# The beginning of a fused feed-forward, attention, feed-forward kernel in another order: the first tiles' statistics ahead, down's transposes behind tile 0, a share of the copies and the output bias on VectorE

## The chip, the cores and the metric

The kernel runs on one core of one Trainium2 chip. The metric is the device time of one execution in microseconds; for the kernel before there are three such runs. A trace of one further execution, the profiled one, is what the rows below come from. Engines: PE is TensorE, DVE is VectorE, ACT is ScalarE, POOL is GpSimd, SP is SyncE, which only issues DMAs.

## What is computed

The input x has 16 x 1024 rows of 256 columns, in float32. The layer is a sandwich: half a feed-forward block, attention, half a feed-forward block with the same weights.

```python
def fp4_quant_dequant(x):
    xb = x.reshape(shape[:-1] + (shape[-1] // BLOCK, BLOCK))     # BLOCK = 16
    scale = jnp.max(jnp.abs(xb), axis=-1, keepdims=True) / 6.0
    scale = jnp.maximum(scale, jnp.float32(1e-12))
    xn = xb / scale
    idx = jnp.searchsorted(_MID, jnp.abs(xn))
    q = _GRID[idx] * jnp.sign(xn) * scale
...
gate = fp4_linear(x, w_gate)            # 256 -> 704, x and w quantized
y = fp4_linear(x, w_up)
h = jax.nn.silu(gate) * y
return fp4_linear(h, w_down)            # 704 -> 256
...
x = x + 0.5 * _L0_ffn_ref(_layernorm(x, axis=-1), w_gate, w_up, w_down)
x = x + _L0_attn_ref(_layernorm(x, axis=-1), Wqkv, bqkv, Wout, bout, gamma, beta)
x = x + 0.5 * _L0_ffn_ref(_layernorm(x, axis=-1), w_gate, w_up, w_down)
```

The attention is a causal linear attention with 16 heads, whose output projection has a bias `bout`. Its weights are prepared at the start of the kernel too.

## The kernel before

The 16384 rows are 128 tiles of 128 rows. All of x stays in SBUF (`x_sb`), and the three stages (`ffn_0`, attention, `ffn_1`) run over all tiles one after the other, with some steps of the next stage woven into the last of the one before (`stages`). Each engine has a program of its own; in it every stage is a sequence of steps, and the engines are bound together by semaphores that count tiles. The order in each engine's program is written by hand.

One step i of the first feed-forward stage works on several tiles at once, since an engine is some steps ahead of another:

- ScalarE (`scalar_step`): silu of tile i (L705), the first rounding "quarter" (L710), sum and squares of tile i+6 (L721, L733), the scale of h of tile i-1 (L729), the second rounding "odd" (L746) and the normalized x of tile i+5 (L748). Before L746 stands the wait for the shift of tile i+5. L710 and L746 treat round i-1, that is h of tile i-1 and x of tile i+3.
- GpSimd (`gpsimd_step`): reciprocal root and shift of tile i+5 (L675, L677, L687), the quantized x of tile i+2 in two fp16 parts (L685, L689) and the quantized h of tile i-2 (L694, L695).
- SyncE (`sync_step`): load of tile i+14, transposition by DMA of quantized x of tile i+2 (L593) and of quantized h of tile i-2 (L599).
- TensorE (`tensor_step`): gate and up of tile i, 18 matmuls (L764), and down of tile i-4, 17 matmuls (L776). There are two sets of PSUM banks for gate and up and one bank for down, so down of tile i-4 waits until tile i-5 is added.
- VectorE (`vector_step`): h of tile i (L614), block maxima, scales and reciprocals of round i, that is h of tile i and x of tile i+4 (L621 to L636), the addition of down's product of tile i-4 (L641), the code q of round i-1 (L648), y = value / scale of round i (L652), and small scales (L655 to L665). L655 is a `tensor_tensor` of two SBUF operands; L652 has one of its operands in PSUM.

The steps begin at -6, and those below 0 do only the part on x. So step 0 of VectorE is the first with an h.

Around these first steps stands the preparation of the weights. `prepare_ffn` quantizes gate, up and down (0, 1, 2) with `scales`, `powers` and `values` on VectorE, `rounds` on ScalarE and `reduce` (a maximum over the partitions, L362) on GpSimd. The value is split in a part "hi" in fp16 (`upper`, ScalarE) and the rest "lo" (`lower`, VectorE, L419 and L417). TensorE transposes both parts in 14 sets of at most six 128 x 128 blocks (`tensor`, L443) into one of four PSUM banks in turn, and ScalarE copies each set into the weights' place in SBUF (`copies`, L460). The first eight sets are gate's and up's, then four of down's hi and two of down's lo. TensorE does all sets before its step -6.

`prepare_attention` centres the weights of q, k and v on GpSimd (`centre`, L1330 to L1333), takes their maxima on VectorE (`tops`, L1353) and over the partitions on GpSimd (`reduce`, L1363), forms powers of two (`powers`, VectorE), the hi part (`upper`, ScalarE, L1386), the lo part (`lower`, VectorE, L1392), and splits the output bias in three bf16 rows (`bias_rows`, GpSimd, L1404 to L1415: eleven dependent instructions, ten of them on 3 x 256 elements). Four DMAs on SyncE transpose the attention weights (`turn`, L1295).

The order is that of the five `block` functions below; the places of interest are where `of_ffn...` and `of_attn...` calls stand between `in_order(engine, ffn_step, first, end)`, which are the steps first to end - 1.

## Time and profile before

| what | us |
|---|---|
| three runs | 2251.57, 2252.20, 2253.18 (median 2252.2) |
| the profiled execution's own time | 2248.39 |
| its span in the trace | 2246.7 |
| busy in the span: TensorE, VectorE, GpSimd, ScalarE | 2127.5, 2055.7, 1902.1, 1849.2 |

The span runs from the first to the last instruction of the trace; 1.7 us of the execution's time lie around it. The page gives averages over three stages and the beginning; what happens in the first 100 us is read from the timelines of each engine, and what it means for the end from the busy time by stretches. Busy time of an engine counts neither its waits nor the issue of DMAs.

### The profile page before, as it was taken

To read this page: it belongs to the slowest core of one execution; us is meant where nothing else is said; L and a number is where in the kernel's file an instruction comes from. 1 tells how busy PE (TensorE), PEld (TensorE's weight loads), DVE (VectorE), ACT (ScalarE), POOL (GpSimd) and SP (SyncE) were. 2 spreads that over 40 slices of the span, in tenths; PEclk is the share of its full clock that TensorE was granted. 3 is DMA by queue.
4 is the path that set the end of the run, shared out by engine and by line. 5 is a ranking of instruction groups with operands and counts; after the bars stand their busy time and mean duration, and the time that the engine had idled before them with its cause. 6 is when DMAs were issued, how large, how long until landed. Compare 5 with 4: busy or idle time off the path is not lost.

```text
span 2246.7 us, 91266 instructions
## 1 busy us (share of the span) xinstructions
PE 2127.5 (95%) x30414; PEld 1495.2 (67%) x30414; DVE 2055.7 (92%) x5219; ACT 1849.2 (82%) x3888; POOL 1902.1 (85%) x3009
## 2 busy tenths in 40 slices
PE   1799999999999889999999999978999999999998
PEld 1466666666666578888888888864666666566665
DVE  6799999999999779999999999978999999999997
ACT  5788888888888678888888888867888888888885
POOL 2899999999999768888888888868998999999896
...
GB/s 95 96 115 117 113 111 117 116 111 114 117 113 97 86 65 72 72 72 72 72 72 72 72 72 72 74 52 71 113 111 111 113 113 115 111 113 111 111 115 118
DMA packets 735774, 216.32 MB, mean 96 GB/s; under 512 B 665952, under 2 KB 735456, under 8 KB 735712
## 3 DMA queue, kind: packets, MB, share of 16 engines
...
q8 instruction: 30, 0.49, 0.1%
q14 instruction: 32, 0.26, 0.0%
...
## 4 chain that ended last, share of the span: by engine, by line
DVE 42%; PE 21%; issue 13%; POOL 11%; DMA 4%; SPq 4%; DVEq 2%; ACT 2%; POOLq 0%; ACTq 0%
DVE ffn_y L652 10%; DVE ffn_per_block L621 9%; DVE ffn_hx L614 8%; PE ffn_ps_gu L764 5%; PE attn_ps_qk L1157 4%; DMA attn_xT<-attn_x_hl 4%; DVE ffn_q L648 3%; PE ffn_ps_down L776 3%; POOL ffn_h_hl L695 2%; PE attn_ps_num L1196 2%; POOL ffn_h_hl L694 2%; PE attn_ps_v_second L1173 2%; SPq L939 2%; DVE ffn_scale L627 2%; DVE ffn_x_scale_lo L655 1%
## 5 line engine op out<-in xcount | busy, mean ns | idle before, releaser
L764 PE MATMUL ffn_ps_gu<-wgu_hi,ffn_xT 128*128 128x512 f16 (+1 forms) x3072 | 737.1, 363 | 27.8 <-DMA ffn_xT<-ffn_x_hl 24.8
L764 PEld LDWEIGHTS ffn_ps_gu<-wgu_hi,ffn_xT 128*128 128x128 f16 x3072 | 300.6, 98 | 314.0 <-issue 20.3
L710 ACT ACTIVATE ffn_quarter<-ffn_y,offsets 128x960 int16<-128x960 f32 (+2 forms) x264 | 282.7, 1071 | 183.6 <-DVE ffn_y L652 183.6
L764 PE MATMUL ffn_ps_gu<-wgu_lo,ffn_xT 128*128 128x512 f16 (+1 forms) x1536 | 431.0, 362 | 0.0
L776 PE MATMUL ffn_ps_down<-wd_hi,ffn_hT 128*128 128x256 f16 x2816 | 349.9, 273 | 17.9 <-DVE x_sb L641 13.2
L694 POOL TENSOR_TENSOR ffn_h_hl<-ffn_q,ffn_h_scale_hi 128x704 f16<-128x704 f16 x256 | 351.8, 1374 | 13.8 <-DVE ffn_h_scale_lo L658 10.6
L695 POOL TENSOR_TENSOR ffn_h_hl<-ffn_q,ffn_h_scale_lo 128x704 f16<-128x704 f16 x256 | 354.7, 1386 | 0.0
L776 PEld LDWEIGHTS ffn_ps_down<-wd_hi,ffn_hT 128*128 128x128 f16 x2816 | 264.4, 98 | 99.5 <-issue 35.7
L621 DVE TENSOR_REDUCE ffn_per_block<-ffn_hx 128x60 f32<-128x960 f32 (+2 forms) x264 | 298.4, 1130 | 24.1 <-ACT ffn_hx L748 1.8
L652 DVE TENSOR_TENSOR ffn_y<-ffn_hx,ffn_per_block 128x960 f32<-128x960 f32 (+2 forms) x264 | 294.9, 1117 | 0.3 <-issue 0.3
L746 ACT ACTIVATE ffn_odd<-ffn_quarter,offsets 128x960 f16<-128x960 int16 (+2 forms) x264 | 278.7, 1056 | 19.4 <-POOL ffn_shift L687 19.4
L614 DVE SCALAR_TENSOR_TENSOR ffn_hx<-ffn_ps_gu,unscale,ffn_silu 128x704 f32<-128x704 f32 x256 | 243.4, 951 | 17.1 <-issue 10.7
L764 PEld LDWEIGHTS ffn_ps_gu<-wgu_lo,ffn_xT 128*128 128x128 f16 x1536 | 150.6, 98 | 154.9 <-issue 1.7
L705 ACT ACTIVATE ffn_silu<-ffn_ps_gu,unscale 128x704 f32<-128x704 f32 x256 | 212.1, 828 | 20.1 <-PE ffn_ps_gu L764 20.0
L685 POOL TENSOR_TENSOR ffn_x_hl<-ffn_q,ffn_x_scale_hi 128x256 f16<-128x256 f16 x256 | 158.2, 618 | 68.2 <-POOL ffn_rstd L677 40.4
L776 PE MATMUL ffn_ps_down<-wd_lo,ffn_hT 128*128 128x256 f16 x1536 | 210.2, 273 | 0.0
L1157 PE MATMUL attn_ps_qk<-attn_xT,attn_w_hi 128*128 128x128 f16 x2048 | 180.1, 220 | 18.5 <-DMA attn_xT<-attn_x_hl 16.0
L677 POOL TENSOR_TENSOR ffn_rstd<-ffn_rstd,minus_half 128x1 f32<-128x1 f32 x256 | 166.9, 652 | 20.0
L689 POOL TENSOR_TENSOR ffn_x_hl<-ffn_q,ffn_x_scale_lo 128x256 f16<-128x256 f16 x256 | 160.1, 625 | 20.0
L776 PEld LDWEIGHTS ffn_ps_down<-wd_lo,ffn_hT 128*128 128x128 f16 x1536 | 150.6, 98 | 17.7
L1157 PEld LDWEIGHTS attn_ps_qk<-attn_xT,attn_w_hi 128*128 128x128 f16 x2048 | 134.2, 98 | 40.9 <-DMA attn_xT<-attn_x_hl 29.1
L748 ACT ACTIVATE ffn_hx<-x_sb,ffn_shift,ffn_rstd 128x256 f32 (+1 forms) x256 | 150.0, 586 | 8.6 <-POOL ffn_shift L687 8.6
...
## 6 DMA issues: line engine op xcount, KB each, us to landing
attn_v_eo<-attn_v_nat SPq DMA_DIRECT2D x512, 34.0 KB, 1.9
x_sb<-in_L_attn_x SPq DMA_DIRECT2D x128, 128.0 KB, 2.3
out<-x_sb SPq DMA_DIRECT2D x128, 128.0 KB, 2.1
ffn_xT<-ffn_x_hl SPq DMA_TRANSPOSE x256, 2.4
ffn_hT<-ffn_h_hl SPq DMA_TRANSPOSE x256, 3.5
attn_xT<-attn_x_hl SPq DMA_TRANSPOSE x128, 2.4
attn_oT<-attn_o_hl SPq DMA_TRANSPOSE x128
...
```

The costliest lines, as they stand in the source:

```text
L614: nc.vector.scalar_tensor_tensor(hx[par][:, 0:INNER], ps_gu[par][:, INNER:2 * INNER], unscale[:, 1:2], silu[:], ALU.mult, ALU.mult).then_i ...
L621: nc.vector.tensor_reduce(amax[:, blocks_in(front)], blocks(hx[par][:, front]), AXX, ALU.max, apply_absolute_value=True).then_inc(S["amax" ...
L652: nc.vector.tensor_tensor(blocks(y[:, front]), blocks(hx[par][:, front]), over_block(inv[:, at], at.stop - at.start), ALU.mult).then_inc(S ...
L677: nc.gpsimd.tensor_tensor(rstd[oth][:], rstd[oth][:], minus_half[:, 0:1], ALU.pow).then_inc(S["rstd"], 1)
L694: nc.gpsimd.tensor_tensor(blocks(h_hl[par][:, 0:INNER]), blocks(q[par][:, 0:INNER]), over_block(h_scale_hi[par][:], HB), ALU.mult)
L695: nc.gpsimd.tensor_tensor(blocks(h_hl[par][:, INNER:]), blocks(q[par][:, 0:INNER]), over_block(h_scale_lo[par][:], HB), ALU.mult).then_inc ...
L705: nc.scalar.activation(silu[:], ps_gu[par][:, 0:INNER], ACT.Silu, scale=unscale[:, 0:1]).then_inc(S["silu"], 1)
L710: nc.scalar.activation(quarter[:, back], y[:, back], ACT.Identity, bias=offsets[:, 0:1], scale=4.0 / HALF_MIN).then_inc(S["quarter"], 1)
L746: nc.scalar.activation(odd[:, back], quarter[:, back], ACT.Identity, bias=offsets[:, 1:2], scale=HALF_MIN / 4.0).then_inc(S["odd"], 1)
L764: last = nc.tensor.matmul(ps_gu[par][:, a:b], xT[par][:, c, :], w[:, k, a:b], start=(n == 0), stop=(n == len(terms) - 1))
L776: last = nc.tensor.matmul(ps_down[:, 0:D], hT[par][:, c, :], w[:, c, :], start=(n == 0), stop=(n == len(terms) - 1))
L1157: last = nc.tensor.matmul(ps_qk[:, col, :], w[:, col, k], aT, start=(n == 0), stop=(n == len(terms) - 1))
```

## The change

The work stays the same but for three points: the copy of down's hi part is shorter (L409 copies its first 64 columns of each chunk instead of all 704, and the sets read the first copy where they can), the lo sets are copied by VectorE instead of ScalarE, and the output bias is split by VectorE in nine instructions instead of eleven on GpSimd. The rest is order:

- GpSimd centres the attention weights after step -4 instead of before step -6, and takes the attention maximum after step -2 instead of after step -4.
- TensorE turns gate's and up's sets, does steps up to 0, turns down's sets, and goes on with step 1. Hi and lo sets have two banks each, placed behind the three banks of tile 0's gate and up.
- ScalarE copies hi sets only, and its `upper` calls and copies stand one or more steps later.
- VectorE copies the lo sets of gate after `powers`, those of up after `values` of down, those of down after step -2, and only then takes the attention maxima. The attention's lo part comes between steps 0 and 1, the output bias between 1 and 2.
- SyncE does its four weight transpositions before steps 2 to 5 instead of 1 to 4.

```diff
@@ -174,11 +174,10 @@
             ffn_step(sp, -14, 0)
             of_ffn.load_down(sp)
             of_attn.load(sp)
-            in_order(sp, ffn_step, -13, 1)
+            in_order(sp, ffn_step, -13, 2)
             for k in range(4):
                 of_attn.turn(sp, k)
-                ffn_step(sp, 1 + k, (1 + k) % 2)
-            in_order(sp, ffn_step, 5, FIRST)
+                ffn_step(sp, 2 + k, k % 2)
             of_ffn.drained(sp)
             of_attn.turned(sp)
             stages(sp, N, ffn_step, of_attn_steps.sync, of_ffn_1.sync, 14)
@@ -195,16 +194,23 @@
             of_ffn.lower(dve, 0)
             of_ffn.values(dve, 1)
             of_ffn.powers(dve, 2, 3)
+            of_ffn.copies_lo(dve, 0, 2)
+            in_order(dve, ffn_step, -6, -3)
             of_ffn.lower(dve, 1)
             of_ffn.values(dve, 2)
-            in_order(dve, ffn_step, -6, -3)
+            of_ffn.copies_lo(dve, 2, 4)
+            in_order(dve, ffn_step, -3, -2)
             of_ffn.lower(dve, 2)
+            in_order(dve, ffn_step, -2, -1)
+            of_ffn.copies_lo(dve, 4, 6)
             of_attn.tops(dve)
-            in_order(dve, ffn_step, -3, -2)
+            in_order(dve, ffn_step, -1, 0)
             of_attn.powers(dve)
-            in_order(dve, ffn_step, -2, -1)
+            in_order(dve, ffn_step, 0, 1)
             of_attn.lower(dve)
-            in_order(dve, ffn_step, -1, FIRST)
+            in_order(dve, ffn_step, 1, 2)
+            of_attn.bias(dve)
+            in_order(dve, ffn_step, 2, FIRST)
             stages(dve, N, ffn_step, of_attn_steps.vector, of_ffn_1.vector)
 
         @block.gpsimd
@@ -215,12 +221,10 @@
             of_ffn.reduce(pool, 0)
             of_ffn.reduce(pool, 1)
             of_ffn.reduce(pool, 2)
+            in_order(pool, ffn_step, -6, -3)
             of_attn.centre(pool)
-            in_order(pool, ffn_step, -6, -3)
+            in_order(pool, ffn_step, -3, -1)
             of_attn.reduce(pool)
-            in_order(pool, ffn_step, -3, -2)
-            in_order(pool, ffn_step, -2, -1)
-            of_attn.bias(pool)
             in_order(pool, ffn_step, -1, FIRST)
             stages(pool, N, ffn_step, of_attn_steps.gpsimd, of_ffn_1.gpsimd)
 
@@ -233,24 +237,28 @@
             of_ffn.upper(act, 0)
             in_order(act, ffn_step, -6, -5)
             of_ffn.rounds(act, 2)
-            of_ffn.copies(act, 0, 2)
+            in_order(act, ffn_step, -5, -4)
             of_ffn.upper(act, 1)
-            of_ffn.copies(act, 2, 4)
-            in_order(act, ffn_step, -5, -4)
+            of_ffn.copies_hi(act, 0, 2)
+            in_order(act, ffn_step, -4, -3)
+            of_ffn.copies_hi(act, 2, 4)
+            in_order(act, ffn_step, -3, -2)
             of_ffn.upper(act, 2)
-            of_ffn.copies(act, 4, 8)
-            in_order(act, ffn_step, -4, -3)
-            of_ffn.copies(act, 8, None)
-            in_order(act, ffn_step, -3, -2)
+            in_order(act, ffn_step, -2, -1)
+            of_ffn.copies_hi(act, 4, 8)
+            in_order(act, ffn_step, -1, 1)
             of_attn.upper(act)
-            in_order(act, ffn_step, -2, FIRST)
+            in_order(act, ffn_step, 1, FIRST)
             stages(act, N, ffn_step, of_attn_steps.scalar, of_ffn_1.scalar)
 
         @block.tensor
         def _(pe):
-            of_ffn.tensor(pe)
-            in_order(pe, of_ffn_0.tensor, -6, FIRST)
-            stages(pe, N, of_ffn_0.tensor, of_attn_steps.tensor, of_ffn_1.tensor)
+            ffn_step = of_ffn_0.tensor
+            of_ffn.tensor_gate_up(pe)
+            in_order(pe, ffn_step, -6, 1)
+            of_ffn.tensor_down(pe)
+            in_order(pe, ffn_step, 1, FIRST)
+            stages(pe, N, ffn_step, of_attn_steps.tensor, of_ffn_1.tensor)
 
 
 @dataclass
@@ -322,16 +332,19 @@
-        hi_down = sb([P, DC * HL], F16).rearrange("p (c h) -> p c h", c=DC)
+        hi_down = sb([P, DC * (INNER + SUB)], F16).rearrange("p (c h) -> p c h", c=DC)
...
+        scope.enter_context(nc.psum_tensor("ps_first_tile", [P, 3, 512]))
         ps = scope.enter_context(nc.psum_tensor("ps_prep", [P, 4, 1024], F16))
@@ -406,7 +419,7 @@
             act.wait_ge(val_ready, w + 1)
             if w == DOWN:
                 nc.scalar.activation(hi_down[:, :, 0:INNER], by_chunk(w), ACT.Copy)
-                nc.scalar.activation(hi_down[:, :, INNER:], by_chunk(w), ACT.Copy).then_inc(hi_ready, 1)
+                nc.scalar.activation(hi_down[:, :, INNER:], by_chunk(w)[:, :, 0:SUB], ACT.Copy).then_inc(hi_ready, 1)
             else:
                 nc.scalar.activation(hi[w], raw[w], ACT.Copy).then_inc(hi_ready, 1)
 
@@ -419,30 +432,48 @@
                 nc.vector.tensor_tensor(lo[w], raw[w], hi[w], ALU.subtract).then_inc(lo_ready, 1)
 
 
...
+        GU_SETS = 2 * len(GATE_UP)
+        copied = (hi_copied, lo_copied)
+
+        def bank(n, s):
+            return ps[:, 2 * n + s % 2]
+
+        def turn_sets(pe, n, first, end):
+            for s in range(first, end):
+                part, src, _ = sets[n][s]
+                pe.wait_ge((hi_ready, lo_ready)[n], part)
+                if s >= 2:
+                    pe.wait_ge(copied[n], s - 1)
+                for j, a in enumerate(src):
+                    last = nc.tensor.transpose(bank(n, s)[:, j * P:(j + 1) * P], a, ident16[:])
+                last.then_inc((hi_turned, lo_turned)[n], 1)
+
+        def tensor_gate_up(pe):
             pe.wait_ge(ident_done, 4)
-            for s, (part_ready, n_part, src, _) in enumerate(sets):
-                pe.wait_ge(part_ready, n_part)
-                if s >= 4:
-                    pe.wait_ge(t_copied, s - 3)
-                for j, a in enumerate(src):
-                    last = nc.tensor.transpose(ps[:, s % 4, j * P:(j + 1) * P], a, ident16[:])
-                last.then_inc(t_done, 1)
-            pe.wait_ge(t_copied, len(sets))
+            for w in GATE_UP:
+                for n in range(2):
+                    turn_sets(pe, n, 2 * w, 2 * w + 2)
+            for n in range(2):
+                pe.wait_ge(copied[n], GU_SETS)
+
+        def tensor_down(pe):
+            for n in range(2):
+                turn_sets(pe, n, GU_SETS, len(sets[n]))
+            drained(pe)
 
...
@@ -452,18 +483,26 @@
             act.wait_ge(quarter_ready, w + 1)
             nc.scalar.activation(odd[w], quarter[w], ACT.Identity, bias=offsets[:, 1:2], scale=HALF_MIN / 4.0).then_inc(odd_ready, 1)
 
-        def copies(act, first, end):
-            for s in range(first, end or len(sets)):
-                act.wait_ge(t_done, s + 1)
-                src, dst = sets[s][2:]
-                from_ps = ps[:, s % 4, 0:len(src) * P]
-                nc.scalar.activation(dst, from_ps.rearrange("p (t c j) -> p c t j", c=DC, j=SUB) if s < GU_SETS else from_ps, ACT.Copy).then_inc(t_copied, 1)
+        def from_bank(n, s):
+            part = bank(n, s)[:, 0:len(sets[n][s][1]) * P]
+            return part.rearrange("p (t c j) -> p c t j", c=DC, j=SUB) if s < GU_SETS else part
+
+        def copies_hi(act, first, end):
+            for s in range(first, end):
+                act.wait_ge(hi_turned, s + 1)
+                nc.scalar.activation(sets[0][s][2], from_bank(0, s), ACT.Copy).then_inc(hi_copied, 1)
+
+        def copies_lo(dve, first, end):
+            for s in range(first, end):
+                dve.wait_ge(lo_turned, s + 1)
+                nc.vector.tensor_copy(sets[1][s][2], from_bank(1, s)).then_inc(lo_copied, 1)
 
...
@@ -1391,28 +1430,17 @@
             dve.wait_ge(hi_ready, w + 1)
             nc.vector.scalar_tensor_tensor(lo[:, at], raw_all[:, at], up2[:, w:w + 1], hi[:, at], ALU.mult, ALU.subtract).then_inc(split, 1)
 
-    def bias_rows(pool):
-        n_part = 0
-
-        def then(ins):
-            nonlocal n_part
-            n_part += 1
-            ins.then_inc(part_step, 1)
-            pool.wait_ge(part_step, n_part)
-
-        pool.wait_ge(z_up_ready, 1)
-        nc.gpsimd.tensor_scalar(eps2[:, 1:2], z_up, LN_EPS, z_up, ALU.mult, ALU.mult).then_inc(done, 1)
-        pool.wait_ge(zero_rows, 1)
-
-        then(nc.gpsimd.tensor_scalar(spare, rows[0:3, 0, :], z_up[0:3], None, ALU.mult))
+    def bias_rows(dve):
+        dve.wait_ge(zero_rows, 1)
+        mark(nc.vector.tensor_scalar(eps2[:, 1:2], z_up, LN_EPS, z_up, ALU.mult, ALU.mult))
+
+        then(dve, nc.vector.tensor_scalar(spare, rows[0:3, 0, :], z_up[0:3], None, ALU.mult))
         for k in range(2):
-            then(nc.gpsimd.tensor_copy(part3[k], spare))
-            then(nc.gpsimd.tensor_tensor(spare, spare, part3[k], ALU.subtract))
-        then(nc.gpsimd.tensor_scalar(rest[0], part3[0], ident[0:3, 0:1], None, ALU.mult))
-        then(nc.gpsimd.tensor_scalar(rest[1], part3[1], ident[0:3, 1:2], None, ALU.mult))
-        then(nc.gpsimd.tensor_scalar(spare, spare, ident[0:3, 2:3], None, ALU.mult))
-        then(nc.gpsimd.tensor_tensor(rest[0], rest[0], rest[1], ALU.add))
-        nc.gpsimd.tensor_tensor(bout3[0:3, :], rest[0], spare, ALU.add).then_inc(done, 1)
+            then(dve, nc.vector.tensor_copy(part3[k], spare))
+            then(dve, nc.vector.tensor_tensor(spare, spare, part3[k], ALU.subtract))
+        then(dve, nc.vector.tensor_scalar(rest, part3[0], ident[0:3, 0:1], None, ALU.mult))
+        then(dve, nc.vector.scalar_tensor_tensor(rest, part3[1], ident[0:3, 1:2], rest, ALU.mult, ALU.add))
+        nc.vector.scalar_tensor_tensor(bout3[0:3, :], spare, ident[0:3, 2:3], rest, ALU.mult, ALU.add).then_inc(done, 1)
 
     return AttentionWeights(load, gpsimd, masks, centre, tops, reduce, powers, upper, lower, bias_rows, turn, turned)
 
```

How the compiled programs show it. The place on which most rests is VectorE's program around the attention maxima. L621 to L655 are the parts on x of one step; the x_sb operands are the area of x_sb that serves as scratch. Before, from step -4's last instructions on:

```order
L652 TENSOR_TENSOR ffn_y<-ffn_hx_61,ffn_per_block 128x256
L655 TENSOR_TENSOR ffn_x_scale_lo_72<-ffn_scale_63,ffn_x_scale_hi_70 128x16
L417 TENSOR_TENSOR x_sb<-x_sb 128x2x704
L1348 TENSOR_REDUCE attn_even<-attn_diag 128x1
L1349 TENSOR_REDUCE x_sb<-attn_diag 128x4
L1350 TENSOR_TENSOR attn_own<-attn_diag 128x8
L1353 TENSOR_REDUCE x_sb<-x_sb 128x1 x2
```

And now, from the end of step -2 on, on the same engine:

```order
L691 TENSOR_TENSOR ffn_y<-ffn_hx_61,ffn_per_block 128x256
L694 TENSOR_TENSOR ffn_x_scale_lo_72<-ffn_scale_63,ffn_x_scale_hi_70 128x16
L498 COPY wd_lo<-ps_prep 128x768 x2
L1387 TENSOR_REDUCE attn_even<-attn_diag 128x1
L1388 TENSOR_REDUCE x_sb<-attn_diag 128x4
L1389 TENSOR_TENSOR attn_own<-attn_diag 128x8
L1392 TENSOR_REDUCE x_sb<-x_sb 128x1 x2
```

The maxima (L1353, now L1392) moved behind two more steps and behind the two copies of down's lo sets.

The second place is TensorE's beginning; before:

```order
L443 MATMUL ps_prep<-ident,x_sb 128x128 x78
L764 MATMUL ffn_ps_gu<-wgu_hi,ffn_xT_88 128x512 x4
L764 MATMUL ffn_ps_gu<-wgu_lo,ffn_xT_88 128x512 x2
L764 MATMUL ffn_ps_gu<-wgu_hi,ffn_xT_88 128x512 x4
L764 MATMUL ffn_ps_gu<-wgu_lo,ffn_xT_88 128x512 x2
```

and now:

```order
L462 MATMUL ps_prep<-ident,x_sb 128x128 x44
L803 MATMUL ffn_ps_gu<-wgu_hi,ffn_xT_88 128x512 x4
L803 MATMUL ffn_ps_gu<-wgu_lo,ffn_xT_88 128x512 x2
L803 MATMUL ffn_ps_gu<-wgu_hi,ffn_xT_88 128x512 x4
L803 MATMUL ffn_ps_gu<-wgu_lo,ffn_xT_88 128x512 x2
L803 MATMUL ffn_ps_gu<-wgu_hi,ffn_xT_88 128x384 x4
L803 MATMUL ffn_ps_gu<-wgu_lo,ffn_xT_88 128x384 x2
L462 MATMUL ps_prep<-ident,x_sb 128x128 x34
```

The 34 transposes of down's sets moved behind tile 0's gate and up.

The third place is GpSimd around the attention maximum. Before, between the shift of tile 1 (step -4) and that of tile 2 (step -3):

```order
L687 TENSOR_SCALAR ffn_shift_59<-ffn_neg_mean_53,ffn_rstd_57 128x1
L1363 ISA
L1363 ISA x_sb<-x_sb 128x2
L675 ISA
L675 TENSOR_TENSOR ffn_rstd_56<-ffn_var_54,eps 128x1
```

and now, behind the quantized x of tile 0 (step -2), ahead of step -1:

```order
L728 TENSOR_TENSOR ffn_x_hl_84<-ffn_q_68,ffn_x_scale_lo_72 128x256
L1402 ISA
L1402 ISA x_sb<-x_sb 128x2
L714 ISA
L714 TENSOR_TENSOR ffn_rstd_56<-ffn_var_54,eps 128x1
```

The maximum with its two extra ISA instructions moved two steps back, from ahead of tile 0's quantized x to behind it. Lines L1402 and L714 are L1363 and L675 of before.

## Rows read from the trace of the kernel before

**Rows 1.** The page: span, busy time by engine, the costliest groups (columns below).
```profile
span 2246.7 us, 91266 instructions
...
PE 2127.5 (95%) x30414; PEld 1495.2 (67%) x30414; DVE 2055.7 (92%) x5219; ACT 1849.2 (82%) x3888; POOL 1902.1 (85%) x3009
...
L694 POOL TENSOR_TENSOR ffn_h_hl<-ffn_q,ffn_h_scale_hi 128x704 f16<-128x704 f16 x256 | 351.8, 1374 | 13.8 <-DVE ffn_h_scale_lo L658 10.6
```

**Rows 2.** Busy time by stretch; heads: stretch, its us, busy us of each engine.
```profile
core 0: us, PE busy (x) PEld busy (x) DVE busy (x) ACT busy (x) POOL busy (x), PEclk, DMA share, GB/s
90.00:120.00 30.00, 28.43 (x184) 17.46 (x182) 28.75 (x75) 25.71 (x54) 27.71 (x42) 1.00 0.74 128
120.00:700.00 580.00, 578.67 (x3718) 360.98 (x3716) 549.41 (x1380) 500.93 (x1066) 531.83 (x744) 1.00 0.56 114
```

**Rows 3.** Timeline of TensorE: start, us, line, operation, [idle before <-releaser].
```profile
20.34 1.33 PE L443 MATMUL ps_prep<-ident,x_sb 128*128 128x128 f16 x11 [20.34 <-ACT x_sb L411]
...
58.44 1.87 PE L764 MATMUL ffn_ps_gu<-wgu_hi,ffn_xT 128*128 128x512 f16 x4 [12.51 <-DMA ffn_xT<-ffn_x_hl]
...
62.96 0.49 PE L764 MATMUL ffn_ps_gu<-wgu_lo,ffn_xT 128*128 128x384 f16 x2
...
96.02 1.36 PE L776 MATMUL ffn_ps_down<-wd_hi,ffn_hT 128*128 128x256 f16 x11 [0.83 <-DVE x_sb L641]
```

**Rows 4.** Timeline of VectorE, 24 to 96 us.
```profile
24.55 0.52 DVE L398 TENSOR_SCALAR x_sb<-x_sb 128x1408 int16<-128x1408 int16 x1
...
25.28 1.63 DVE L400 TENSOR_TENSOR x_sb<-x_sb 128x1408 f32<-128x1408 f16 x1
...
28.79 1.62 DVE L419 TENSOR_TENSOR x_sb<-x_sb 128x1408 f16<-128x1408 f32 x1 [1.19 <-ACT x_sb L411]
30.33 3.06 DVE L398 TENSOR_SCALAR x_sb<-x_sb 128x1408 int16<-128x1408 int16 x1
...
37.00 0.43 DVE L621 TENSOR_REDUCE ffn_per_block<-ffn_hx 128x16 f32<-128x256 f32 x1 [1.77 <-ACT ffn_hx L748]
...
37.96 0.42 DVE L652 TENSOR_TENSOR ffn_y<-ffn_hx,ffn_per_block 128x256 f32<-128x256 f32 x1
...
41.14 0.15 DVE L1348 TENSOR_REDUCE attn_even<-attn_diag 128x1 f32<-128x4 f32 x1
...
60.37 2.47 DVE L1392 SCALAR_TENSOR_TENSOR x_sb<-x_sb 128x1536 f16<-128x1536 f32 x2
...
71.27 0.95 DVE L614 SCALAR_TENSOR_TENSOR ffn_hx<-ffn_ps_gu,unscale,ffn_silu 128x704 f32<-128x704 f32 x1 [1.84 <-ACT ffn_silu L705]
...
76.76 0.95 DVE L614 SCALAR_TENSOR_TENSOR ffn_hx<-ffn_ps_gu,unscale,ffn_silu 128x704 f32<-128x704 f32 x1 [0.86 <-PE ffn_ps_gu L764]
...
81.98 0.95 DVE L614 SCALAR_TENSOR_TENSOR ffn_hx<-ffn_ps_gu,unscale,ffn_silu 128x704 f32<-128x704 f32 x1
...
92.39 0.95 DVE L614 SCALAR_TENSOR_TENSOR ffn_hx<-ffn_ps_gu,unscale,ffn_silu 128x704 f32<-128x704 f32 x1
...
95.40 0.48 DVE L641 SCALAR_TENSOR_TENSOR x_sb<-ffn_ps_down,ffn_h_unscale,x_sb 128x256 f32<-128x256 f32 x1
```

**Rows 5.** The chain of waits: start, us, what.
```profile
36.06 0.28 POOL ffn_shift L687
...
52.62 0.28 POOL ffn_shift L687
```

**Rows 6.** Timeline of GpSimd, 28 to 67 us.
```profile
28.85 4.16 POOL L1330 TENSOR_TENSOR x_sb<-x_sb 128x1530 f32<-128x1530 f32 x1 [7.81 <-issue]
...
43.83 0.38 POOL L1363 PARTITION_ALL_REDUCE x_sb<-x_sb  x1 [6.22 <-DVE x_sb L1353]
51.65 0.18 POOL L675 TENSOR_TENSOR ffn_rstd<-ffn_var,eps 128x1 f32<-128x1 f32 x1 [7.45 <-issue]
...
54.92 0.62 POOL L689 TENSOR_TENSOR ffn_x_hl<-ffn_q,ffn_x_scale_lo 128x256 f16<-128x256 f16 x1
...
66.10 0.18 POOL L675 TENSOR_TENSOR ffn_rstd<-ffn_var,eps 128x1 f32<-128x1 f32 x1
```

**Rows 7.** Timeline of ScalarE: the copies from PSUM.
```profile
39.40 1.38 ACT L460 ACTIVATE wgu_hi<-ps_prep 128x768 f16<-128x768 f16 x2
```

More of the change, by code:

```diff
@@ L278 @@
     rounds: Callable
-    copies: Callable
-    tensor: Callable
+    copies_hi: Callable
+    copies_lo: Callable
+    tensor_gate_up: Callable
+    tensor_down: Callable
     drained: Callable
@@ L1259, in prepare_attention @@
     bias = sb([P, QT])
-    spare, *rest = [sb([3, D]) for _ in range(3)]
+    spare, rest = [sb([3, D]) for _ in range(2)]
     part3 = [sb([3, D], BF16) for _ in range(2)]
```

25 lines of the change are left out of this document (13 added, 12 removed).

## The prediction

> **What bounds the kernel now.** I read four views. The page first [rows 1]: TensorE is busy 95% of the span, VectorE 92%, and the profiled execution has a span of 2246.7 us. Then the busy time by stretch [rows 2]: from 120 to 700 us, the first feed-forward stage, TensorE is busy 578.67 of 580 us, VectorE 549.41. So from about 96 us on, TensorE has no idle time to give back, while VectorE has some 0.28 us of slack in a step of 5.4 us. All that the change touches lies before that. The end can therefore move only by the amount by which TensorE's unbroken run begins earlier or later. That beginning can be seen in TensorE's rows [rows 3]: the last wait is at 96.02, when the product with down's weights for tile 1 waits 0.83 us for VectorE's L641 (tile 0 added), which starts at 95.40 in VectorE's step 4 [rows 4]. Step 4 began at 92.39. So **the start of VectorE's step 4 is what counts**: a shift of it passes whole to the end.
>
> The chain of waits [rows 5] and GpSimd's rows [rows 6], the next two views, tell what made step 4 start at 92.39. GpSimd's cross-partition maximum at 43.83 is followed by 7.45 us in which the engine waits for nothing shown, before L675 at 51.65; the same gap, 7.81 us, stands before 28.85. It is the switch from the maximum's code to the ordinary operations: the compiled program has an extra ISA instruction at just these places. Then come shift (L687), tile 0's quantized x (L689, until 55.54), the output bias (L1404 to L1415, most of the time from 55.54 on), and at 66.10 step -1. Silu of tile 0 waits for this step's shift, and VectorE's first step, 0, starts at 71.27. I call the time from 66.10 to 71.27 (5.17 us) the tail.
>
> **The change, term by term.** Times without another word are positions on the span's clock, and durations are from [rows 3, 4, 5, 6].
>
> 1. *Tile 0 earlier.* GpSimd no longer centres the attention weights first. Its switch still ends at 28.85, shift takes 1.24 us (51.65 to the end of L687 at 52.89), and from shift's end to VectorE's L621 there are 0.66 us (36.34 to 37.00). Step -4 on VectorE starts at 30.8 instead of 37.0. Quantized x of tile 0 (L689's end, call it X) follows later, through VectorE: tile 0's last small operation waits for the centring on GpSimd, then up's rest (1.6 us as at 28.79), down's values (L398, L399, L400: 2.3 us), two copies, step -3 to the code q (1.2 us: 37.00 to 37.96 and a short L648), and 1.7 us on GpSimd. The centring itself is 2.7 us: the row shows 4.16, but VectorE's L419 ran until 30.4, and L398, due at 30.33, took 3.06 instead of 0.52 us, until 33.4, when centring ended. The two engines exclude each other here. So the centring ends at 34.1 and VectorE's chain gives 34.1 + 0.1 + 1.6 + 2.3 + 1.3 + 1.2 + 1.8 = 42.4. If GpSimd's four small instructions alternate with VectorE's, 1.4 us more: 43.8. I take **X = 43.1**, 12.4 us earlier than 55.54.
>
> 2. *Copies on VectorE.* No row shows VectorE copying 768 two-byte elements from PSUM. Below, the fast int16 rows bound it (0.52 us for 1408, so 0.35); above, L614 (0.95 us for 704 columns from PSUM, so 1.0). The same copy on ScalarE takes 0.69 [rows 7]; I take 0.65, pairs 1.3 us, which stands in term 1 and again in 3.
>
> 3. *What now stands behind tile 0.* This is the heart. VectorE's attention maxima (the reading of L1353) now stand behind two copies of down's rest, these behind TensorE's transposes for down, these behind tile 0's gate and up products, these behind X. From X: 2.9 us to the first product (55.54 to 58.44), 5.0 us for the products (to 63.45; the first four take 1.87 us). Then 34 transposes in six sets with only two banks per part, at 0.73 us a set as in the row at 20.34 (1.33 for 11), or perhaps 0.45 once warm; ScalarE's copies at 0.64 lie between. Set 4, a copy, sets 6, 7 and the first set of the rest, then two copies on VectorE: 4.05 to 4.9 us, I take 4.3. The maxima start at 43.1 + 2.9 + 5.0 + 4.3 = 55.3. From their start to the end of the switch back is 10.51 us today (41.14 to 51.65). GpSimd's step -1 starts at **65.8**, against 66.10: the bias's ten microseconds are gone, and the switch has taken their place. VectorE idles some 8 us before the copies, which costs nothing by itself. The tail is unchanged (step -1 on VectorE and the powers, 1.7 us, just fit), so step 0 starts at **71.0** instead of 71.27.
>
> 4. *New work between VectorE's steps.* Step 0 ends 4.6 us after its start (76.76 less its 0.86 us of waiting, less 71.27). Now the attention rest follows (2.4 us, at 60.37 it hid in idle time) and waits about 0.2 us for a GpSimd instruction. Step 1: 71.0 + 4.6 + 0.2 + 2.4 = 78.2 instead of 76.76. TensorE's tile 1 is no later than now. Step 1 takes 5.2 us (76.76 to 81.98). Then the bias: one tiny operation and eight of 256 columns. Alone, by 0.42 us of L652's 256 columns, 0.15 + 8 × 0.40 = 3.4 us. But GpSimd is then in tile 0's h, two instructions of 1.37 us [rows 1], and the dependent operations of VectorE must each find a gap. If the two-input ones wait, 5.6 us. I take 4.5; floor 2, if each costs no more than a 16-column operation. Step 2: 78.2 + 5.2 + 4.5 = **87.9** instead of 81.98.
>
> 5. *To step 4.* Steps 2 and 3 take 10.4 us and VectorE has hardly a gap in them, so step 4 is at 98.3 instead of 92.39: **+5.9 us**. TensorE's own delay for tile 4's products would be only some 2 us, but it meets L641 at the next step. The four weight transposes by DMA on SP move one step back; they fall where TensorE waits for VectorE anyway: nothing.
>
> Sum: 2248.39 + 5.9 = 2254.3 for the profiled execution; the median of the three runs, 2252.2, lies 3.8 us above the profiled execution's 2248.39, so **2258.1 us** to compare with 2252.2.
>
> **A rule beside the row.** For the switch the row says 7.45 us. The Trainium skill, GPSIMD Engine Reference, section Instruction dispatch, puts the loading of a new kernel's code at about 6 us. By that the sum would be 1.5 us less, 2256.6; the row decides.
>
> **The rivals.**
>
> *TensorE covers it (22%).* VectorE's slack and TensorE's two gate/up banks might absorb the new work: if tile 1's down product does not wait on step 4, only the first tile's shift counts, -0.3 to +1.4 us, and the time is 2252.9. For it: VectorE is 5% idle in the stage. Against it: the 0.83 us behind L641 today. Cheap bias (2 us) with X at 42.4 would also end near it, at +2.7.
>
> *Port alternation (20%).* GpSimd and VectorE exclude each other for whole instructions, as L398's 3.06 us shows. If every bias operation wants the port, one-source ones too, it costs 6.9 us: 3.4 of its own, 2 × 1.37 of h and about 0.8 of small GpSimd work. With X at 43.8 and slow transposes (4.9) the shift is 5.9 + 2.4 + 0.7 + 0.6 = +9.6: 2261.8. The Trainium skill, SBUF — State Buffer, section Who interferes with whom, says the pair is taken for a whole instruction, by one-source operations in a two-port mode too. The trace agrees for L398.
>
> *The other side: the switch does not gate (8%).* If the code switch behind the maximum were already paid or ran during the wait, step -1 would start 7.4 us earlier, at 58.4, and tile 0's gain would arrive: step 0 at 63.6. It decides if the gap after the maximum is under 2 us. With the attention rest and a bias of 2 us, hidden in part while TensorE is still behind, the shift is -7.4 + 1.4 + 2 - 2 = about -6: 2246.2. Against it: two gaps of 7.45 and 7.81 us in one trace.
>
> **How the numbers follow.** The forecast's own case has 50%, from +3.5 to +8 us. Some 0.2% (4.5 us) is what a measurement of this kernel tells from no change, so slower by more: 47 of the 50, and the port rival's 20: 0.67. Within: 3 of the forecast, 22 of the cover, 1 of the last: 0.26. Faster: 0.07. The range leaves out the last rival and the upper half of the port one: 2251.5 to 2262.
>
> **What would show it.** Right: GpSimd idle 7 to 8 us behind the attention maximum, its next step at 65 to 67; VectorE idle for 6 us or more before the copies of down's rest; the first L614 form near 71, the second near 78, the third 86 to 90; TensorE as full as now from about 102 on. Wrong: the third h before 85, a down product for tile 1 that waits for no VectorE operation, or a gap behind the maximum of under 5 us.

## The result and the profile after

| | kernel before | changed kernel |
|---|---|---|
| median of the runs, us | 2252.2 (7 runs, 2250.59 to 2254.73) | 2260.7 (7 runs, 2258.83 to 2262.96) |
| profiled execution, us | 2248.39 | 2261.47 |
| its span, us | 2246.7 | 2259.8 |

The ratio is 1.0037, with a 95% interval from 1.0025 to 1.0048: slower by 8.5 us. The forecast was 5.9 us slower, 2258.1, range 2251.5 to 2262.0. The direction and the range held; the size was 2.6 us short.

The page and the busy time by stretch of the changed kernel, which answer to [rows 1, 2]:

```profile
span 2259.8 us, 91266 instructions
...
PE 2128.1 (94%) x30414; PEld 1495.4 (66%) x30414; DVE 2067.0 (91%) x5234; ACT 1844.7 (82%) x3882; POOL 1882.9 (83%) x2998
```

```profile
76.00:79.00 3.00, 3.00 (x8) 1.03 (x7) 2.90 (x8) 2.97 (x7) 0.74 (x2) 0.50 0.47 126
90.00:120.00 30.00, 24.97 (x141) 14.39 (x142) 28.78 (x70) 21.85 (x45) 23.36 (x34) 0.89 0.65 120
94.40:97.00 2.60, 2.60 (x7) 0.95 (x8) 2.53 (x7) 0.79 (x1) 0.17 (x1) 0.50 0.62 122
97.00:99.40 2.40, 2.40 (x7) 0.82 (x6) 2.33 (x7) 1.57 (x4) 2.24 (x4) 0.50 0.00 0
120.00:700.00 580.00, 578.86 (x3719) 361.06 (x3717) 549.42 (x1380) 501.14 (x1066) 531.66 (x745) 1.00 0.57 114
```

The long stage is as it was, with TensorE at 578.86 of 580 us; from 90 to 120 us TensorE is busy 3.5 us less than before. (The short stretches are for the clock, the third number from the end; they are used in the last section.) So what the change itself costs is lost in the beginning; what else the two profiled executions differ by is told under "What counts". VectorE's timeline, answering to [rows 4], from the copies of down's rest to the end of step 4's addition:

```profile
59.29 1.02 DVE L498 COPY wd_lo<-ps_prep 128x768 f16<-128x768 f16 x2 [14.68 <-PE ps_prep L462]
60.23 0.15 DVE L1387 TENSOR_REDUCE attn_even<-attn_diag 128x1 f32<-128x4 f32 x1
...
75.77 0.95 DVE L653 SCALAR_TENSOR_TENSOR ffn_hx<-ffn_ps_gu,unscale,ffn_silu 128x704 f32<-128x704 f32 x1
...
80.32 2.74 DVE L1431 SCALAR_TENSOR_TENSOR x_sb<-x_sb 128x1536 f16<-128x1536 f32 x2
82.99 0.94 DVE L653 SCALAR_TENSOR_TENSOR ffn_hx<-ffn_ps_gu,unscale,ffn_silu 128x704 f32<-128x704 f32 x1
...
87.87 0.20 DVE L1435 TENSOR_SCALAR attn_eps<-x_sb 128x1 f32<-128x1 f32 x1
...
88.37 1.34 DVE L1439 CAST x_sb<-x_sb 3x256 bf16<-3x256 f32 x1
89.74 1.49 DVE L1440 TENSOR_TENSOR x_sb<-x_sb 3x256 f32<-3x256 f32 x1
91.26 0.28 DVE L1439 CAST x_sb<-x_sb 3x256 bf16<-3x256 f32 x1
91.58 0.41 DVE L1440 TENSOR_TENSOR x_sb<-x_sb 3x256 f32<-3x256 f32 x1
...
93.31 0.93 DVE L653 SCALAR_TENSOR_TENSOR ffn_hx<-ffn_ps_gu,unscale,ffn_silu 128x704 f32<-128x704 f32 x1
...
103.26 0.95 DVE L653 SCALAR_TENSOR_TENSOR ffn_hx<-ffn_ps_gu,unscale,ffn_silu 128x704 f32<-128x704 f32 x1
...
106.27 0.48 DVE L680 SCALAR_TENSOR_TENSOR x_sb<-ffn_ps_down,ffn_h_unscale,x_sb 128x256 f32<-128x256 f32 x1
```

L653 is L614 of before. Steps 0, 1, 2 and 4 begin at 75.77, 82.99, 93.31 and 103.26, against 71.27, 76.76, 81.98 and 92.39: +4.5, +6.2, +11.3 and +10.9. The attention rest (L1431) and the bias (L1435 to L1443) stand between the steps as the order says. GpSimd's timeline, answering to [rows 6]:

```profile
31.50 2.74 POOL L1369 TENSOR_TENSOR x_sb<-x_sb 128x1530 f32<-128x1530 f32 x1
...
41.10 0.62 POOL L728 TENSOR_TENSOR ffn_x_hl<-ffn_q,ffn_x_scale_lo 128x256 f16<-128x256 f16 x1
62.91 0.37 POOL L1402 PARTITION_ALL_REDUCE x_sb<-x_sb  x1 [21.18 <-DVE x_sb L1392]
70.51 0.18 POOL L714 TENSOR_TENSOR ffn_rstd<-ffn_var,eps 128x1 f32<-128x1 f32 x1 [7.23 <-issue]
...
88.15 1.42 POOL L733 TENSOR_TENSOR ffn_h_hl<-ffn_q,ffn_h_scale_hi 128x704 f16<-128x704 f16 x1
89.53 1.43 POOL L734 TENSOR_TENSOR ffn_h_hl<-ffn_q,ffn_h_scale_lo 128x704 f16<-128x704 f16 x1
```

Tile 0's quantized x ends at 41.72, 13.8 us earlier than before, and then GpSimd waits 21.18 us for VectorE's maxima. Behind the maximum stands the gap of 7.23 us, and step -1 starts at 70.51 instead of 66.10. TensorE, answering to [rows 3]:

```profile
49.93 1.86 PE L803 MATMUL ffn_ps_gu<-wgu_hi,ffn_xT 128*128 128x512 f16 x4 [12.72 <-DMA ffn_xT<-ffn_x_hl]
...
52.45 1.91 PE L803 MATMUL ffn_ps_gu<-wgu_hi,ffn_xT 128*128 128x512 f16 x4
...
56.34 0.83 PE L462 MATMUL ps_prep<-ident,x_sb 128*128 128x128 f16 x12
...
94.39 1.86 PE L803 MATMUL ffn_ps_gu<-wgu_hi,ffn_xT 128*128 128x512 f16 x4 [5.85 <-DVE ffn_hx L653]
...
106.89 1.36 PE L815 MATMUL ffn_ps_down<-wd_hi,ffn_hT 128*128 128x256 f16 x11 [0.55 <-DVE x_sb L680]
```

The last wait is the same one as before, at 106.89 instead of 96.02: +10.87, as step 4. And why is the first product at 49.93, 8.2 us after its x was there? SyncE's queue tells:

```profile
21.37 25.67 SPq L620 DMA_DIRECT2D x_sb<-in_L_attn_x  x12
47.23 1.32 SPq L632 DMA_TRANSPOSE ffn_xT<-ffn_x_hl  x1
```

Tile 0's transposition (L632) stands behind twelve loads of x, which take until 47.04, 2.14 us each on average. It is the kernel that spaces them: SyncE's program waits at each load until the one before has landed (`load`, L619: eleven waits, 20.7 us together). The transposition's input was ready at 41.72, and it was issued at 47.23. In the kernel before, the same queue:

```profile
21.31 24.84 SPq L581 DMA_DIRECT2D x_sb<-in_L_attn_x  x12
55.72 1.33 SPq L593 DMA_TRANSPOSE ffn_xT<-ffn_x_hl  x1
```

There the loads were through at 46.15, and x, at 55.54, was the later one.

### The profile page after: what moved, and what is told of

It reads as the page before. It is cut to its first block, busy times and chain, and to the rows that moved or that the text cites. A ratio compares the mean times of both kernels' runs of the same rounds, so it can differ in the third digit from the quotient of the medians.

```text
span 2259.8 us, 91266 instructions
## 1 busy us (share of the span) xinstructions
PE 2128.1 (94%) x30414; PEld 1495.4 (66%) x30414; DVE 2067.0 (91%) x5234; ACT 1844.7 (82%) x3882; POOL 1882.9 (83%) x2998
## 4 chain that ended last, share of the span: by engine, by line
DVE 42%; PE 20%; issue 15%; POOL 12%; DMA 4%; SPq 4%; DVEq 2%; ACT 1%; POOLq 0%; ACTq 0%
DVE ffn_y L691 10%; DVE ffn_per_block L660 8%; DVE ffn_hx L653 7%; PE ffn_ps_gu L803 5%; PE attn_ps_qk L1196 4%; DVE ffn_q L687 4%; POOL ffn_h_hl L734 3%; DMA attn_xT<-attn_x_hl 3%; POOL ffn_h_hl L733 3%; PE ffn_ps_down L815 3%; PE attn_ps_num L1235 2%; SPq L978 2%; PE attn_ps_v_second L1212 2%; DVE ffn_scale L666 2%; DVE ffn_x_scale_lo L694 1%
## 5 line engine op out<-in xcount | busy, mean ns | idle before, releaser
L733 POOL TENSOR_TENSOR ffn_h_hl<-ffn_q,ffn_h_scale_hi 128x704 f16<-128x704 f16 x256 | 351.2, 1372 | 14.4 <-DVE ffn_h_scale_lo L697 10.5
L734 POOL TENSOR_TENSOR ffn_h_hl<-ffn_q,ffn_h_scale_lo 128x704 f16<-128x704 f16 x256 | 353.9, 1383 | 0.0
L653 DVE SCALAR_TENSOR_TENSOR ffn_hx<-ffn_ps_gu,unscale,ffn_silu 128x704 f32<-128x704 f32 x256 | 243.3, 950 | 14.3 <-issue 10.4
```

What stands on the lines that cost most here:

```text
L653: nc.vector.scalar_tensor_tensor(hx[par][:, 0:INNER], ps_gu[par][:, INNER:2 * INNER], unscale[:, 1:2], silu[:], ALU.mult, ALU.mult).then_i ...
L733: nc.gpsimd.tensor_tensor(blocks(h_hl[par][:, 0:INNER]), blocks(q[par][:, 0:INNER]), over_block(h_scale_hi[par][:], HB), ALU.mult)
L734: nc.gpsimd.tensor_tensor(blocks(h_hl[par][:, INNER:]), blocks(q[par][:, 0:INNER]), over_block(h_scale_lo[par][:], HB), ALU.mult).then_inc ...
```

## The experiments

"D4" is the start of VectorE's step 4 (the fifth L614 form), which the prediction held to pass whole to the end. Each kernel was timed in five rounds beside the kernel before, whose median was 2251.4 to 2251.7 there (2252.2 beside the changed kernel). D4 and step 0 are those of one profiled execution of each kernel, the medians those of all its runs.

| kernel | median | ratio (95%) | step 0 | D4 | D4 against 92.39 | median against before |
|---|---|---|---|---|---|---|
| changed kernel | 2260.7 | 1.0037 (1.0025 to 1.0048) | 75.77 | 103.26 | +10.9 | +8.5 |
| maxima ahead of the copies | 2249.7 | 0.9991 (0.9982 to 1.0000) | 62.53 | 90.03 | -2.4 | -1.7 |
| transposition ahead | 2256.1 | 1.0021 (1.0012 to 1.0030) | 69.68 | 97.18 | +4.8 | +4.7 |
| before, bias on VectorE | 2246.6 | 0.9977 (0.9968 to 0.9986) | 68.61 | 88.78 | -3.6 | -4.7 |
| weights in the gap | 2241.1 | 0.9956 (0.9942 to 0.9969) | 62.18 | 82.48 | -9.9 | -10.3 |
| gap and transposition | 2241.7 | 0.9953 (0.9940 to 0.9967) | 61.39 | 83.37 | -9.0 | -9.9 |
| no switch | 2252.2 | 1.0002 (0.9993 to 1.0011) | 66.69 | 94.18 | +1.8 | +0.5 |
| bias behind step 5 | 2261.4 | 1.0040 (1.0026 to 1.0053) | 73.13 | 95.65 | | +9.8 |

**The maxima ahead of the copies.** This undoes one part: what if the maxima did not wait for TensorE?

```diff
-            of_ffn.copies_lo(dve, 4, 6)
             of_attn.tops(dve)
+            of_ffn.copies_lo(dve, 4, 6)
             in_order(dve, ffn_step, -1, 0)
```

> The changed kernel, with the attention maxima ahead of the copies of down's rest on VectorE (two calls exchanged). Theory A, the code switch behind the cross-partition maximum gates the first h, and the start of VectorE's step 4 passes whole to the end: the maxima start at 44.6 instead of 60.3, GpSimd's maximum at 47.1, its step -1 at 54.8 instead of 70.5; the first h is then held by ScalarE's copies (until 59.5) and starts at 64 to 65 instead of 75.8, VectorE's step 4 at 92 instead of 103.3; time 11 us under the changed kernel, 2249.5. Theory B, the loss is the new work on VectorE between steps 0 and 2 alone: this work stays, so the time stays within 2 us of 2260.7 though the first h is earlier. Theory C, the loss is TensorE's cold clock after long idle times: idle times stay (step 3's products still wait for the third h), time within 3 us of 2260.7.

Measured: 2249.7 us, D4 90.03. GpSimd's maximum moved from 62.91 to 47.13, and 11 us of the time went with it:

```profile
47.13 0.37 POOL L1402 PARTITION_ALL_REDUCE x_sb<-x_sb  x1 [5.90 <-DVE x_sb L1392]
55.16 0.18 POOL L714 TENSOR_TENSOR ffn_rstd<-ffn_var,eps 128x1 f32<-128x1 f32 x1 [7.66 <-issue]
```

Step 0 was at 62.53, 2 us earlier than expected, and the time was as expected. So the place of two lines turns the change from a loss of 8.5 us into a gain of 1.7, at the edge of what can be told.

**The transposition ahead.** SyncE issues tile 0's transposition behind ten loads instead of twelve; it tests the term that the prediction lacks. With `loads=False` a step leaves out its load, with `turns=False` its transposition.

```diff
-            in_order(sp, ffn_step, -13, 2)
+            in_order(sp, ffn_step, -13, -3)
+            ffn_step(sp, -2, 0, loads=False)
+            ffn_step(sp, -3, 1)
+            ffn_step(sp, -2, 0, turns=False)
+            in_order(sp, ffn_step, -1, 2)
...
```

> The changed kernel, with tile 0's transposition issued on SyncE after ten of the twelve loads of x instead of after all twelve. Theory A, what I had left out of the sum is SyncE's queue: twelve loads, one each 2.07 us from 21.3 on, stand ahead of tile 0's transposition, which was ready to go at 41.8 but was issued at about 47: now issued at 42, first product at 44.7 instead of 49.9, VectorE's maxima, GpSimd's switch, the first h and step 4 all 5.2 us earlier, time 2255.5. Rival, the transposition is slow for another reason (DMA engines busy with the loads, the DMA itself takes 8 us): the first product moves by less than 2 us and the time by less than 2.

Measured: 2256.1 us. SyncE's queue shows the edit:

```profile
20.83 20.46 SPq L624 DMA_DIRECT2D x_sb<-in_L_attn_x  x10
41.49 1.32 SPq L636 DMA_TRANSPOSE ffn_xT<-ffn_x_hl  x1
```

The first product came at 44.68 instead of 49.93, D4 6.1 us earlier and the median 4.6. Without this term the changed kernel is 4.7 us slower than before, where the prediction, which did not have the term, said 5.9.

**The kernel before, with its bias on VectorE.** It takes GpSimd's ten microseconds away and gives VectorE the change's nine instructions, behind the attention rest; the order of all else is that of before.

```diff
             of_attn.lower(dve)
+            of_attn.bias(dve)
             in_order(dve, ffn_step, -1, FIRST)
...
             of_attn.reduce(pool)
             in_order(pool, ffn_step, -3, -2)
-            in_order(pool, ffn_step, -2, -1)
-            of_attn.bias(pool)
-            in_order(pool, ffn_step, -1, FIRST)
+            in_order(pool, ffn_step, -2, FIRST)
...
```

> The kernel before, with one part of the change: the output bias split by VectorE (nine instructions) behind the attention's lo part, before step -1, instead of by GpSimd. Theory A: GpSimd's step -1 follows step -2 at 56 instead of 66.1, VectorE does the bias in time in which it waited; first h at 62 instead of 71.3, VectorE's step 4 at 83 to 84 instead of 92.4, time 9 us under before: 2243. Theory B, bias work on VectorE costs its 5.4 us wherever it stands: at best 4 us under before, 2248.

Measured: 2246.6 us; faster, but by 4.7 us where twice that was expected. GpSimd's step -1 came at 59.57 instead of 66.10, held by another wait, and then VectorE itself was the later one:

```profile
59.57 0.19 POOL L674 TENSOR_TENSOR ffn_rstd<-ffn_var,eps 128x1 f32<-128x1 f32 x1 [3.75 <-ACT ffn_squares L732]
...
61.17 1.66 POOL L686 TENSOR_SCALAR ffn_shift<-ffn_neg_mean,ffn_rstd 128x1 f32<-128x1 f32 x1
...
65.18 0.85 ACT L704 ACTIVATE ffn_silu<-ffn_ps_gu,unscale 128x704 f32<-128x704 f32 x1
...
63.29 0.20 DVE L1395 TENSOR_SCALAR attn_eps<-x_sb 128x1 f32<-128x1 f32 x1
...
68.61 0.94 DVE L613 SCALAR_TENSOR_TENSOR ffn_hx<-ffn_ps_gu,unscale,ffn_silu 128x704 f32<-128x704 f32 x1
```

ScalarE's squares (L732) had the attention's hi part ahead of them, and shift took 1.66 instead of 0.27 us beside VectorE's attention rest (60.49 to 63.37). Silu was ready at 66.03, but VectorE was in its bias from 63.29 to 66.91 and then in its part of step -1, and came to step 0 at 68.61 without an idle moment. So GpSimd's bias was a limit of the kernel before, and at this place VectorE had no waiting time left in which to do the work instead: the 3.6 us of its bias stand on the path.

**The bias late.** On VectorE it stands behind step 5 instead of between 1 and 2 (FIRST is 6).

```diff
-            in_order(dve, ffn_step, 1, 2)
+            in_order(dve, ffn_step, 1, FIRST)
             of_attn.bias(dve)
-            in_order(dve, ffn_step, 2, FIRST)
             stages(dve, N, ffn_step, of_attn_steps.vector, of_ffn_1.vector)
```

> The changed kernel with VectorE's output bias behind its step 5 instead of between steps 1 and 2; all else as changed. Two theories of what 5.4 us of new work on VectorE cost. (a) Wherever the work stands among VectorE's steps it is paid in full, because VectorE's own chain sets when TensorE's unbroken run begins and has no cushion afterwards: the h operation of step 4 starts 5.4 us earlier (97.8 instead of 103.3), but behind step 5 TensorE waits some 5 us for VectorE a second time; total within 1.5 us of the changed kernel's 2260.7, I say 2260. (b) Once TensorE runs without a break it has two banks of gate and up in hand and covers the bias: total about 2255.5, 5 us less. The 0.55 us wait of the down product behind VectorE's addition today speaks for (a).

Measured: 2261.4 us, near the 2260 of theory (a) and not the 2255.5 of (b). D4 is 7.6 us earlier than in the changed kernel (5.4 of the bias and 2.6 of an earlier step 0 in this execution, with 0.4 given back), and TensorE stands still at another place:

```profile
99.27 1.36 PE L814 MATMUL ffn_ps_down<-wd_hi,ffn_hT 128*128 128x256 f16 x11 [0.81 <-DVE x_sb L679]
...
115.96 2.53 PE L814 MATMUL ffn_ps_down<-wd_hi,ffn_hT 128*128 128x256 f16 x11 [5.68 <-DVE x_sb L679]
```

From D4 to the end of the span it is 2163.8 us here and 2156.5 in the changed kernel: 7.2 us more, for a bias that took 5.8 (106.45 to 112.24). This settles the rival by which TensorE covers new work among VectorE's steps: it does not, early or late. The start of step 4 is a measure of the end only as long as nothing new comes on VectorE behind it.

**No switch.** GpSimd's attention maximum becomes an ordinary copy. This kernel leaves out the maximum over the partitions, so its attention weights are scaled wrongly; all other work is the same.

```diff
-        nc.gpsimd.partition_all_reduce(gtop, top, P, RMAX).then_inc(gtop_ready, 1)
+        nc.gpsimd.tensor_copy(gtop, top).then_inc(gtop_ready, 1)
```

> The changed kernel in which GpSimd's maximum over the partitions of the attention weights is replaced by an ordinary copy of the same two columns. The maximum over partitions of the attention's weights is left out, so each partition scales by its own maximum; the number and size of all other operations stay. Theory (the code switch gates the tail): GpSimd's step -1 follows the copy within half a microsecond, at 63.3 instead of 70.51; first h at 68.5 instead of 75.77, step 4 at 96.0 instead of 103.3, total 2260.7 less 7.3 = 2253.4. Rival (the switch's gap only covers another wait, such as ScalarE's squares or tile 0's gate and up): first h moves by under 2 us, total 2259 or more.

Measured: 2252.2 us, 8.5 less than the changed kernel, against 7.3 expected:

```profile
61.33 0.18 POOL L1402 COPY x_sb<-x_sb 128x2 f32<-128x2 f32 x1 [19.94 <-DVE x_sb L1392]
61.48 0.19 POOL L714 TENSOR_TENSOR ffn_rstd<-ffn_var,eps 128x1 f32<-128x1 f32 x1
```

Step -1 follows at once, 9.0 us earlier. Of these, 1.5 are the copies, which started at 57.78 instead of 59.29: the first product came 0.5 us earlier in this execution, and TensorE sped up 1.0 us sooner. The rest is the gap and the maximum. The gap did stand on the path.

**The weights in the gap.** VectorE idles 14.68 us ahead of down's copies. Here maxima, powers, bias and attention rest all go there (and ScalarE's attention hi part ahead of its own copies):

```diff
             in_order(dve, ffn_step, -2, -1)
-            of_ffn.copies_lo(dve, 4, 6)
             of_attn.tops(dve)
-            in_order(dve, ffn_step, -1, 0)
             of_attn.powers(dve)
-            in_order(dve, ffn_step, 0, 1)
-            of_attn.lower(dve)
-            in_order(dve, ffn_step, 1, 2)
             of_attn.bias(dve)
-            in_order(dve, ffn_step, 2, FIRST)
+            of_attn.lower(dve)
+            of_ffn.copies_lo(dve, 4, 6)
+            in_order(dve, ffn_step, -1, FIRST)
...
```

> The changed kernel, with all of the attention's weight work (maxima, powers, output bias, lo part on VectorE, hi part on ScalarE) put ahead of the copies of down's part, into the time in which both engines waited for TensorE. Theory A: as with the maxima first, first h at 64.4; nothing stands between steps 0, 1 and 2 now, so step 1 at 69.6, step 2 at 74.8, step 4 at 85.2 instead of 103.3 (changed) or 92.4 (before); time 7 us under before, 2245. Theory B and C as for the maxima first, but without the new work between the steps: B gives 5.4 + 2.7 = 8 us under the changed kernel, 2252.6, C within 4 us of it.

Measured: 2241.1 us, 10.3 less than before, 19.6 less than the changed kernel and 3.9 less than expected. The bias ran alone from 49.59 to 52.90, 3.31 us, and there was still idle time ahead of the copies:

```profile
49.59 0.21 DVE L1431 TENSOR_SCALAR attn_eps<-x_sb 128x1 f32<-128x1 f32 x1
...
52.90 2.46 DVE L1427 SCALAR_TENSOR_TENSOR x_sb<-x_sb 128x1536 f16<-128x1536 f32 x2
57.23 1.02 DVE L494 COPY wd_lo<-ps_prep 128x768 f16<-128x768 f16 x2 [1.87 <-PE ps_prep L458]
```

This kernel also tells whether the gap behind the maximum is only the maximum's own work, which the kernel without it cannot, since it removes both. Here VectorE's powers (L1402 in this kernel) follow directly and need the maximum's result:

```profile
47.46 0.37 POOL L1398 PARTITION_ALL_REDUCE x_sb<-x_sb  x1 [6.23 <-DVE x_sb L1388]
47.86 0.17 DVE L1402 TENSOR_SCALAR x_sb<-x_sb 128x2 f32<-128x2 f32 x1 [0.95 <-POOL x_sb L1398]
54.93 0.49 POOL L710 TENSOR_TENSOR ffn_rstd<-ffn_var,eps 128x1 f32<-128x1 f32 x1 [7.10 <-issue]
```

VectorE used the result at 47.86, 0.03 us after the maximum's end, while GpSimd's next ordinary operation came 7.10 us after it. So the gap is not the maximum's own work. That it is the loading of code is a reading of the extra ISA instruction at this place; no run shows it as such.

**Both.** The weights in the gap, and the transposition ahead by the edit shown above.

> The kernel with the attention work of VectorE in the gap before down's copies (2241.1 us, first h at 62.18, step 4 at 82.48), and in addition tile 0's transposition issued behind ten of SyncE's loads instead of twelve. Theory: first product of TensorE near 44.5 instead of 49.3, down's copies 5 us earlier; then the first h is gated by GpSimd's step -1 behind the attention maximum's code switch (near 54.9), plus the tail of 5.2 us: first h at 60.1 instead of 62.2, step 4 near 80.4, total 2239. Rival (a): everything still follows the products, first h at 57.5, total 2236.5. Rival (b): the earlier products gain nothing since step 4 hangs on later loads or on tile 1: 2241 again.

Measured: 2241.7 us, no gain over 2241.1; this is the total of rival (b). The first product came 3.4 us earlier (45.94 for 49.29), but GpSimd had become the limit:

```profile
48.42 0.37 POOL L1402 PARTITION_ALL_REDUCE x_sb<-x_sb  x1 [6.72 <-issue]
56.10 0.28 POOL L714 TENSOR_TENSOR ffn_rstd<-ffn_var,eps 128x1 f32<-128x1 f32 x1 [7.32 <-issue]
...
61.52 1.86 PE L803 MATMUL ffn_ps_gu<-wgu_hi,ffn_xT 128*128 128x512 f16 x4 [6.80 <-DMA ffn_xT<-ffn_x_hl]
...
67.74 0.95 DVE L653 SCALAR_TENSOR_TENSOR ffn_hx<-ffn_ps_gu,unscale,ffn_silu 128x704 f32<-128x704 f32 x1 [1.72 <-PE ffn_ps_gu L803]
```

My theory named the right limit for step 0 and put it at 54.9; it stood at 56.10, and step 0 at 61.39 instead of 60.1. Step 0 was still 0.8 us earlier than without the transposition's edit (62.18), but D4 was 0.9 us later (83.37 for 82.48): tile 1's x comes from GpSimd's step -1, so its products started at 61.52 instead of 60.56, and VectorE waited 1.72 us for them at step 1. The transposition's five microseconds count only where TensorE's chain is what the maxima wait for.

## Why the prediction was right, and where its sizes were off

*What counts.* That a shift of D4 passes whole to the end held: over the seven kernels of the table with a value the two last columns differ by 0.1 to 2.4 us. From D4 to the end of the span it is 2156.2 to 2157.9 us in all seven (2259.8 less 103.26 for the changed kernel), and 2154.3 in the profiled execution of before. That one was short, which is part of the reason why the profiled pair differs by 13.1 us and the medians by 8.5. The traces show where: from D4 to the last h of the first stage it is 669.4 to 669.7 us in all eight (762.04 less 92.39 before, 772.67 less 103.26 in the changed kernel), so nothing of the shift is lost there. From that h to the first h of the last stage, the attention, it is 766.1 us in the profiled execution of before (762.04 to 1528.11) and 768.5 to 770.1 in the seven others. Why the attention was shorter in that one execution stays open.

*Term 1, tile 0 earlier.* X was to be 43.1 and was 41.72. The centring was put at 2.7 us once it runs without VectorE's big operations, and took 2.74.

*Term 2, copies on VectorE.* Taken as 0.65 us each, bounds 0.35 to 1.0; two took 1.02, so 0.51.

*Term 3, what stands behind tile 0.* **This is the step that was mis-sized.** "2.9 us to the first product" was read from a trace in which the loads were through before x was ready; it was 8.2 us, +5.3, because of SyncE's twelve loads. The prediction asked what the SyncE queue costs for the four weight transposes alone, and not for the one transposition that the change makes 14 us earlier. The products took 6.4 us (49.93 to 56.34) instead of 5.0, transposes and copies 3.9 instead of 4.3 (the 0.45 us for a fast set of six, for which the prediction had no row, were 0.49). So -1.4 + 5.3 + 1.4 - 0.4 = +4.9: the maxima started at 60.23 instead of 55.3. From there to step -1 it took 10.28 us instead of 10.51, and step 0 was at 75.77 instead of 71.0. That the bias goes and the switch takes its place was right, as the kernel without the switch shows.

*Term 4, new work between steps.* Step 0 to step 1 took 7.22 us, forecast 7.2, and step 1 took 4.88 instead of 5.2. The bias took 5.44 us instead of 4.5, within the bounds of 2 to 5.6: the first L1439 and L1440 lasted 1.34 and 1.49 us beside GpSimd's L733 and L734, and 0.28 and 0.41 us when they came again. Alone the bias takes 3.31.

*Term 5.* Steps 2 and 3 took 9.95 us instead of 10.4. D4 came out at 103.26 instead of 98.3.

*Why the range held.* D4's shift was 5.0 us more than forecast, the median 2.6 more. The measured +10.9 lies above the forecast's own +3.5 to +8 and above the port rival's +9.6. Had the median moved as D4 did, the time would have been 2252.2 + 10.9 = 2263.1, outside the range that ends at 2262. So the mechanism and the direction were right, and that the time lay within the range was in part luck. The remaining 2.4 us are of the size by which single executions of one kernel differ (4.1 us between the ends of the changed kernel's seven runs); no experiment here resolves them.

*The signs.* Those on the mechanism came: 7.23 us of idle GpSimd behind the attention maximum, 14.68 us of idle VectorE before the copies of down's rest, a down product for tile 1 that waits for VectorE. Those that named a time were all missed by about the same five microseconds: GpSimd's next step at 70.51 and not 65 to 67, TensorE's last wait at 106.89 where it was to be as full as now from about 102 on, the first three h at 75.77, 82.99 and 93.31 and not near 71, near 78 and at 86 to 90. None of the signs of being wrong appeared.

*The two rules.* The rows decided for the longer switch: behind the attention maximum it took 7.23 us here and 6.68 to 7.66 us in the other seven kernels that have it. The Trainium skill (GPSIMD Engine Reference, Instruction dispatch) has about 6 us for loading a kernel's code; each of these gaps is longer. The Trainium skill (SBUF — State Buffer, Who interferes with whom) says that one side holds the pair for a whole instruction. The trace agrees for L1439: a one-source cast of 3 x 256 elements took 1.34 us beside an operation of 1.42.

*The rivals.* TensorE covers it: refuted twice, by the 0.55 us wait at 106.89 and by the late bias. Port alternation: it happened, in two of nine operations, worth 2.1 us, not in all. The switch does not gate: refuted by the kernel without it, and by the one with the weights in the gap, where the maximum's result was in use 7 us before GpSimd went on.
